# An attention and expert kernel: the scores' factor by ln and exp, joined copies of rows and heads, and a new order of calls on all engines

## What is computed

```python
qh, kh, vh = proj(q, Wq, bq), proj(k, Wk, bk), proj(v, Wv, bv)   # q = layernorm(x), k = v = context
scores = einsum('bhqd,bhkd->bhqk', qh, kh)
D = (norm(qh)[..., :, None] + norm(kh)[..., None, :]) ** 2
scores = alpha * 4.0 * scores / D
x = x + (softmax(scores) @ vh) @ Wo + bo
# then: 8 experts, the best 2 of each token, weights by softmax
x = x + sum over experts of  weight * (gelu(layernorm(x) @ W1 + b1) @ W2 + b2)
```

## Time and profile before

| What | us |
|---|---|
| Median of 3 runs (967.82 to 971.75) | 969.62 |
| The profiled execution's own time | 970.74 |
| Its span, first to last instruction | 968.9 |
| PE busy | 898.1 (93%) |
| PE weight loads busy | 789.8 (82%) |
| DVE busy | 697.2 (72%) |
| ACT busy | 634.5 (65%) |
| POOL busy | 415.5 (43%) |

### The profile page before, as it was taken

One profiled execution on the slowest core, in us unless ns is written; L12 is line 12 of the kernel. 1 busy time (PEld: TensorE's weight loads), 2 busy tenths in 40 slices (PEclk: granted clock), 3 DMA queues, 4 the chain that ended last, 5 costly groups with the idle time before them and its releaser, 6 DMA issues.

```text
span 968.9 us, 30634 instructions
## 1 busy us (share of the span) xinstructions
PE 898.1 (93%) x10701; PEld 789.8 (82%) x10701; DVE 697.2 (72%) x1833; ACT 634.5 (65%) x1236; POOL 415.5 (43%) x540
## 2 busy tenths in 40 slices
PE   3999999998999999989899699899999999999994
PEld 2788887787877877878777589799999999999993
DVE  7677888777987887779768577766666666666662
ACT  3688887787877877878857356455555455554551
POOL 6344456538546565385253532623222232222322
PEclk9799999999999999999979799999999999999998
DMA  5222122314132333253044773443333233332222
GB/s 150 70 72 89 41 83 80 112 41 128 57 99 76 126 123 103 92 171 111 20 139 134 275 273 52 85 93 52 51 52 51 47 52 52 52 51 48 46 30 22
DMA packets 61892, 84.82 MB, mean 88 GB/s; under 512 B 9872, under 2 KB 55312, under 8 KB 59568
## 3 DMA queue, kind: packets, MB, share of 16 engines
q1 hardware_dynamic: 47504, 64.26, 21.0%
q0 software_dynamic: 13296, 18.00, 11.1%
q10 hardware_dynamic: 944, 0.60, 0.2%
HBM read 49.86 MB, written 31.92 MB: 84 GB/s over the span
## 4 chain that ended last, share of the span: by engine, by line
PE 74%; issue 7%; DVE 6%; ACT 6%; POOL 3%; another core or an unknown queue 1%; DMA 1%; DVEq 0%; POOLq 0%; ACTq 0%
PE s_ps L711 10%; PE u_ps L711 10%; PE pv_ps L729 9%; PE gen L729 9%; PE gen L502 5%; PE gen L495 5%; PE s_ps L485 5%; PE u_ps L473 3%; PE pv_ps L519 2%; PE gen L544 2%; ACT pt L827 2%; PE gen L415 2%; PE gen L680 2%; PE gen L418 2%; PE gen L422 1%
## 5 line engine op out<-in xcount | busy, mean ns | idle before, releaser
L1567 POOL DMA_INDIRECT out<-yw,rb x71 | 110.3, 1553 | 269.4 <-DVE yw L1392 253.4
L928 ACT ACTIVATE h<-s_ps,b1t,inv 128x128 f32<-128x128 f32 x288 | 107.8, 457 | 89.6 <-PE s_ps L711 79.3
L928 ACT ACTIVATE h<-u_ps,b1t,inv 128x128 f32<-128x128 f32 x280 | 104.7, 459 | 87.4 <-PE u_ps L711 86.4
L1375 DVE TENSOR_SCALAR hs<-h,hsc 128x512 f16<-128x512 f32 x142 | 69.7, 491 | 120.4 <-ACT h L928 102.0
L827 ACT ACTIVATE pt<-gen,escale 128x512 f32<-128x512 f32 x128 | 86.8, 686 | 50.4 <-PE gen L502 34.5
L1377 DVE SCALAR_TENSOR_TENSOR hs<-h,hsc,hs 128x512 f16<-128x512 f32 x142 | 106.7, 751 | 5.1
L711 PE MATMUL s_ps<-xt,w1s 128*128 128x128 f16 x1728 | 104.8, 220 | 2.2 <-issue 2.2
L1517 POOL DMA_INDIRECT xrec<-rec,idx x64 | 77.8, 1215 | 60.9 <-DVE idx L1229 44.7
L711 PE MATMUL u_ps<-xt,w1s 128*128 128x128 f16 x1680 | 102.5, 220 | 0.9 <-issue 0.9
L711 PEld LDWEIGHTS s_ps<-xt,w1s 128*128 x1728 | 99.8, 99 | 2.8 <-issue 2.3
L729 PE MATMUL pv_ps<-w2s_sb,hs 128*128 x864 | 100.5, 272 | 0.5 <-issue 0.5
(11 more groups left out here) (251 smaller groups left out, 1741.8 us busy)
## 6 DMA issues: line engine op xcount, KB each, us to landing
wl<-L_ffn_W SPq DMA_DIRECT2D x16, 1024.0 KB
rb<-xrec SPq DMA_DIRECT2D x71, 132.5 KB
w2s<-wst SPq DMA_DIRECT2D x8, 1024.0 KB
w2s_sb<-w2s SPq DMA_DIRECT2D x8, 1024.0 KB, 20.4
xin<-x SPq DMA_DIRECT2D x32, 128.0 KB, 3.5
cin<-ctx SPq DMA_DIRECT2D x32, 128.0 KB, 2.1
xres<-x SPq DMA_DIRECT2D x32, 128.0 KB
out<-x SPq DMA_DIRECT2D x30, 128.0 KB, 2.0
```

The source lines that it names most:

```text
L928: ins = act.activation(h32[n % HBANKS][:, m % HB, :], hbank[n % HBANKS][:, o:o + SLOT], ACT.Gelu, scale=inv1[:, bass.ds(ex, 1)].bitcast(F3 ...
L1567: pool.indirect_dma_start(out[:, :], bass.IndirectOffsetOnAxis(ap=rb[j][:, D + NE:D + NE + 1], axis=0), yw[s % 2][:, :], None, compute_op= ...
```

## The change

**Factor.** The queries and keys are no longer made unit vectors. PE L473 now sums norms instead of logs, ACT takes Ln of the sum and then Exp of -2 times that, and DVE multiplies by it (`tensor_tensor` instead of `scalar_tensor_tensor`). A table that holds both functions is named ahead of the loop. Ln and Exp of the squared norms run next to one another (`roots`), and DVE's `norms` (9 instructions) takes the place of 14 in three calls. POOL's `units` is split by batch and waits for the copied queries and keys alone.

**Joined copies.** `rows` copies both batches at once (2 instructions for 4), `heads_back` multiplies with one instruction for two, `weight_exponent` has one copy less. `aq`, `uk` and `kbr` hold both batches; the six small transfers `uk<-kbr` share one semaphore, and `factors(0)` waits for all six.

**Order.** All five loops and `TURNS` are written in another order.

```diff
 TURNS = [
-    ("ex30", -1, "ex30", None), ("ex31", -1, "ex31", None), ("qte0", 0, "qte0", None), ("kte0", 0, "kte0", None),
+    ("ex20", -1, "ex20", None), ("xct0", 1, "xce0", None), ("ex21", -1, "ex21", None), ("wsum", -1, "wcl", None),
...
         def scalar_program(act):
+            act.preload_act_table_set("natural_log_exp_and_others")
...
-            def norm_ln(p):
-                act.wait_ge(*at("mant", p + 1))
-                act.activation(na["ln"][:, :, :], na["mant"][:, :, :].bitcast(F32), ACT.Ln).then_inc(sig("nln"), 1)
-
-            def norm_exp(p):
-                act.wait_ge(*at("ah", p + 1))
-                act.activation(na["y"][:, :, :], na["ah"][:, :, :], ACT.Exp, scale=-1.0).then_inc(sig("ny"), 1)
+            def roots(p):
+                for b in range(2):
+                    act.wait_ge(*at(f"n2{b}", p + 1))
...
+                act.activation(na["ln"][:, :, :], n2[:, :, :], ACT.Ln, bias=tiny[:, :]).then_inc(sig("nln"), 1)
+                act.wait_ge(*at("nln", p + 1))
+                act.activation(na["y"][:, :, :], na["ln"][:, :, :], ACT.Exp, scale=-0.5).then_inc(sig("ny"), 1)
...
-                act.activation(th[h][:, :], u_ps[:, :], ACT.Tanh, scale=0.5).then_inc(sig(f"th{n}"), 1)
+                act.activation(th[h][:, :], u_ps[:, :], ACT.Ln, scale=-0.5 / NORM_SCALE).then_inc(sig(f"th{n}"), 1)
                 act.wait_ge(*at(f"th{n}", p + 1))
-                act.activation(th[h][:, :], th[h][:, :], ACT.Square).then_inc(sig(f"t2{n}"), 1)
+                act.activation(th[h][:, :], th[h][:, :], ACT.Exp, scale=-2.0).then_inc(sig(f"t2{n}"), 1)
...
-                for b in range(2):
-                    sp.wait_ge(*at(f"rowk{b}", p + 1))
-                    if p:
-                        sp.wait_ge(*at(f"su{2 * b + 1}", p))
-                    for s in range(NSPLIT):
+                sp.wait_ge(*at("rowk", p + 1))
+                if p:
+                    sp.wait_ge(*at("u3", p))
+                for s in range(NSPLIT):
+                    for b in range(2):
...
-            def units(p):
-                pool.wait_ge(*at("coef", p + 1))
-                for b in range(2):
+            def units(b, p):
...
-            for it in range(-2, NP + 3):
+            for it in range(-2, NP + 4):
+                if 0 <= it < NP:
+                    units(0, it)
...
                 if 0 <= it + 2 < NP:
                     norm(0, it + 2)
-                if 0 <= it - 2 < NP - 1:
-                    record_low(0, it - 2)
+                    norm(1, it + 2)
                 if 0 <= it < NP:
                     split_max(0, it)
```

More of the change, by code:

```diff
@@ L588, in tensor_program @@
                 if 0 <= it - 1 < NP:
-                    turned(3, 0, it - 1)
-                    turned(3, 1, it - 1)
+                    turned(2, 0, it - 1)
+                if 0 <= it + 1 < NP:
+                    norm(0, it + 1)
+                if 0 <= it - 1 < NP:
+                    turned(2, 1, it - 1)
+                    values(1, it - 1)
+                    weight_sum(it - 1)
                 if 0 <= it < NP:
                     stack(0, it)
+                if 0 <= it - 2 < NP - 1:
+                    logits(0, it - 2)
+                if 0 <= it - 1 < NP:
+                    heads_back(0, it - 1)
+                if 0 <= it - 2 < NP - 1:
+                    turn_y(1, it - 2)
+                if 0 <= it - 1 < NP:
+                    turned(3, 0, it - 1)
                 if 0 <= it - 3 < NP - 1 and it % 2 == 0:
                     ranks(it - 3)
+                if 0 <= it - 2 < NP - 1:
+                    logits(1, it - 2)
+                if 0 <= it - 1 < NP:
+                    values(2, it - 1)
                 if 0 <= it < NP:
+                    scores(0, it)
+                    stack(1, it)
                     factors(0, it)
@@ L643, in tensor_program @@
                 if 0 <= it < NP:
-                    values(1, it)
-                if 0 <= it + 2 < NP:
-                    norm(0, it + 2)
-                if 0 <= it < NP:
-                    turned(2, 1, it)
-                if 0 <= it - 1 < NP - 1:
-                    logits(1, it - 1)
-                if 0 <= it + 2 < NP:
-                    norm(1, it + 2)
-                if 0 <= it < NP:
-                    heads_back(0, it)
-                    values(2, it)
+                    values(0, it)
+                    scores(3, it)
             W1_BYTES = 2 * 2 * DC * H
@@ L1296, in vector_program @@
                     choose(it - 2)
+                if 0 <= it - 1 < NP:
+                    weight_low(it - 1)
                 if 0 <= it + 2 < NP:
                     means(0, it + 2)
-                if 0 <= it - 1 < NP:
-                    weight_low(it - 1)
-                if 0 <= it - 2 < NP - 1 and it % 2:
-                    counts(it - 2)
+                    means(1, it + 2)
                 if 0 <= it < NP:
@@ L1306, in vector_program @@
                     residual(0, it - 1)
+                if 0 <= it < NP:
+                    scores(1, it)
+                if 0 <= it + 1 < NP:
+                    squares(1, it + 1)
+                if 0 <= it - 1 < NP - 1:
                     heads_back(1, it - 1)
                 if 0 <= it + 1 < NP:
-                    squares(1, it + 1)
-                if 0 <= it + 2 < NP:
-                    means(1, it + 2)
-                if 0 <= it < NP:
-                    scores(1, it)
+                    squares(0, it + 1)
+                if 0 <= it - 2 < NP - 1 and it % 2:
+                    counts(it - 2)
+                if 0 <= it + 1 < NP:
+                    norms(it + 1)
                 if 0 <= it - 1 < NP - 1:
@@ L1333, in vector_program @@
                     scores(3, it)
+                    weight_exponent(it)
                 if 0 <= it - 1 < NP - 1:
-                    logits(1, it - 1)
+                    logits(0, it - 1)
+                if 0 <= it < NP:
+                    heads_back(0, it)
             exponent(b1ss[:, :], kb[:, :])
```

352 lines of the change are left out of this document (155 added, 197 removed), and 14 rows, old and new, of the table TURNS.

## The result

The changed kernel took 937.45 us in the median of 4 runs (934.46 to 939.13) where the kernel before took 969.1 (967.82 to 971.75): a ratio of 0.9673, 95% interval 0.9647 to 0.97. Two more comparisons gave 0.9664 (0.9646 to 0.9682) and 0.9706 (0.9658 to 0.9754).

What follows compares the result with a forecast made beforehand. PE's work in a row was taken to bound attention, with 20.2 us of holes in ten pairs falling to 8.8: -11.4, +0.7, -1.0, +1.0, -1.0 give -11.7, so 958 us from a median of 969.62; range 948 to 969.

Steps and rivals of the forecast that it cites:

- the floor of 30.33 a pair: Attention pairs: PE is busy 30.33 us a pair, unchanged; only its holes, 2.02 a pair, can go.
- the table loads at 0: ACT: 32 of 36 table loads go, 41.1 us of its time, but 0 on the path.
- pair 14 at +0.7: Pair 14, where `soon_tables` makes DVE late: hole grows to about 3.8, +0.7 us; the low clock stays.
- the hold: Odd iterations, DVE idle on "remote" beside three scatters in a row: PE's hole, 1.6 before, nearest to 0.34; 1.7 over five.
- rival 3: Slower: POOL becomes the wait of every pair, its chain delayed behind `weight_low`; about 984 us, chance 0.11.
- the 0.34 stays: PE's wait ahead of `weight_sum` in each pair, 0.34 us, remains: 3.4 over ten pairs.
- cover for what follows: ACT: the removed table loads gain 0 on the path themselves but give slack for the rest of the change.
- split_max(0) late by 0.3 to 0.4: POOL's split maxima in even iterations: PE waits 0.3 to 0.4 five times, 2.0 us instead of 7.2.
- rival 2: The wait beside three scatters stays whole, 8 us instead of 1.7: 964 (961 to 967), chance 0.16.
- at most 6 could be gained: Pair 14: the most to gain if its low clock were gone, 6 us; not in the sum.
- Start, pair 15, change of stage: -1.0, -1.0, +1.0: Terms outside the ten pairs: start -1.0 (between -3 and +2), pair 15 -1.0, change of stage +1.0 us.
- The forecast's own test for being wrong: Wrong if PE waits over 1 us for `mhl` or `tw` every pair, remote idle exceeds 2, or Ln well above 1.03.

Runs made afterwards that it cites:

- before_one_table: The kernel before with Exp in place of the norms' Ln (wrong norms), so 32 of 36 table loads go; 965.84 us against 967.65, ratio 0.9982.
- one_table_spaced: The kernel before with Exp in place of the norms' Ln and two of four scatters moved apart; 950.53 us, ratio 0.995.
- loads_apart: The changed kernel with two table loads per pair put back where ACT had gaps of 1.02 and 1.14; 940.04 us, ratio 0.9697.
- changed_third: The changed kernel run again without an edit, in a comparison where the kernel before took 967.65; 938.83 us, ratio 0.9706.

## Why the prediction was right and wrong

**Where the miss lies.** The profiles differ by 36.2, 24.5 more than the forecast's 11.7: 8.3 of this in pair 14, 8.0 in the ten pairs, 3.9 in the change of stage, 3.3 in the first three pairs, 2.7 in the start, less 1.9 in pair 15. The steps that failed are the floor of 30.33 a pair, the table loads at 0 and pair 14 at +0.7; the hold was mis-sized too, the other way.

**Direction, and attention as PE's work with holes: right.** The gain lies in holes, the expert stage did not move, and no wait with POOL as the bound of every pair (rival 3) came.

**"PE's work stays, 30.33 a pair": wrong.** I took busy time for a floor. The same 334 rows of PE are busy for 30.02 in a plain pair before and 29.44 after. The record of a matmul is longer than the distance to the next one, so that a stop shows only with what is beyond its modelled end. Two transposes in a plain pair before, and two like them after, with what follows each (timelines of PE):

```profile
85.12 0.41 PE L404 MATMUL gen<-idf,xn 128*128 128x128 f32 x2
85.64 0.66 PE L527 MATMUL gen<-idf,osb 128*128 128x128 f32 x4
```

```profile
164.58 0.39 PE L403 MATMUL gen<-idf,xn 128*128 128x128 f32 x2
164.81 0.60 PE L495 MATMUL gen<-idf,tw 128*128 128x128 f32 x4
```

The next call starts 0.52 after them before and 0.23 after; of these 0.29 only 0.11 is idle in the rows. What PE waited for there, or whether it waited at all, the rows do not say. In the earlier trace rows the idle ahead of `weight_sum` reads 0.34; removing it gave 0.42. A plain pair fell by 1.03: 0.42 is the loads', and of the other 0.61, which the order gave, PE's idle in before_one_table shows 0.11 (30.05 - 29.94). Ten pairs gained 3.5 of busy time, and against that floor the holes were 2.9 a pair (32.35 - 29.44), not 2.02. The Trainium skill ("Perfetto Trace Analysis", "Identifying the Most-Contended Engine") warns that matmul busy share is a poor measure of how near a kernel is to its roofline, since matmuls are pipelined; 30.02 against 29.44 for the same work agrees that busy time is no floor. The distance from start to start of the same piece of work is what I should have compared.

**"Table loads: on the path 0", and "the 0.34 stays": wrong, one error in two places.** Between 299.56 and the exponential that `weight_sum` waits for stand a load, the Ln and a second load; I had said that the 0.34 names ACT and then kept it. It is worth 0.42 a pair in the old order (before_one_table, one_table_spaced), also in the first three pairs, which I left out of the sum altogether. And as "cover for what follows" the loads' absence at that place is what the new order stands on: with them back there it gives nothing, with them in gaps nearly all (loads_apart).

**split_max(0) late by 0.3 to 0.4: nearly.** PE waits for it in two of the five even pairs, for 0.2 at most. The first scatter starts 0.88 after `weight_low` instead of 0.13 and takes 2.45, not 3.19:

```profile
203.08 2.35 DVE L1254 SCALAR_TENSOR_TENSOR w1s<-wl,wsc,w1s 128x2048 f16<-128x2048 f32 x1
```

```profile
203.96 2.45 POOL L1489 DMA_INDIRECT xrec<-rec,idx  x1 [6.06 <-DVE idx L1206]
```

Both times it ends 0.98 after `weight_low` does. Its length is not its own: by these rows it is held until DVE is done and then takes 0.97. The rule of the Trainium skill ("SBUF — State Buffer", "Who interferes with whom") that I had set against this row would have had it at 0.97 beside `weight_low`; the row still speaks against it. An even pair fell by 2.6 (32.4 to 29.8), 13.1 in five, where the forecast had 5.2: 1.03 of the 2.6 is the lower floor, of which 0.42 is the loads'.

**The hold at 0.34: wrong, rival 2 had it.** I went by pair 15 since fewer loads stood beside it. That was no reason: the changed kernel has only two transfers of SP beside the three scatters, and the hold is there, also in its pair 15. Against a plain pair an odd one takes 1.55 more in the mean, 1.8 before, and spacing the scatters gave 8.0. That the five odd pairs fell by 6.3, just the 8 - 1.7 of the forecast, is luck: the floor fell by 1.03 a pair under a hold that stayed. The forecast named the place and the three scatters; it did not see that the hold comes and goes between comparisons.

**Pair 14, +0.7 with the clock low: wrong by 8.3.** PE stops 0.28 before DVE's `tw` starts, where it had stopped 0.92 before it, so the hole is 1.64; I had it at 3.8. With one short hole for two longer ones the clock held. That "at most 6 could be gained" stood in the text, as a thing not expected.

**Start, pair 15, change of stage: -1.0, -1.0, +1.0 against -3.7, +0.9, -2.9.** The start's 3.7 is in part the luck of that execution: changed_third has it at 47.42. Pair 15 lost by the hold: with the scatters spaced it takes 26.3. The change of stage gained where I had only seen DVE's chain stay; no run takes it apart.

**The forecast's own test for being wrong** (a wait for `mhl` or `tw` of over 1 us in every pair, an Ln well above 1.03) did not come; the Ln takes 1.02. The remote idle of over 2 us did, and was worth what rival 2 said. The other terms were wrong to the other side and larger, so that the time fell below the range and below every rival's.

**A slip in rival 3.** Stalls of 1.7 and 2.7 are 2.2 a pair in the mean, and with the 0.34 and the small gaps 2.7, not 3.1: ten pairs would lose 7, not 11. The rival did not come, so nothing hangs on it.

## What to carry to other kernels

Measure a floor from start to start in a stretch where the engine waits for nothing, not by its busy time. An engine's time costs what it makes late at the tight handover behind it: the same two loads per pair cost 3.8 us in one place and 32 in another, so look for who waits behind an instruction before calling it covered, and shift what can't be removed into a gap. A change that lets PE arrive earlier gives its gain away again at the next fixed wait, and a longer hole can then cost the clock too; remove that wait in the same step.

## What the runs showed of the hardware that I had not expected

- PE was held, and DVE saw its results late (2.68 idle on "remote"), beside three indirect writes issued 1.3 apart by POOL: in the traces of four comparisons, in none of another, and in the sixth, by the time of the kernel before (954.87), most likely not. No two in a row had it beside them. Moving two of the three apart ended it in both orders.
- A DVE copy of 1 x 512 bf16 took 2.54 instead of 0.28 beside a POOL memset of 1.79, which began 0.31 after it, and DVE instructions of 0.22 took up to 1.71 beside POOL's `units`.
- Behind one and the same hole of about 1.65 PE's clock stayed at full speed in some executions and fell to the lower level for a few us in others, which costs 1.6.
